# A recurrent block and a 32-expert layer on one core: first steps reordered, a fifth set of result buffers for expert 7, and both pairs of expert 0 added ahead of the last four scatters

## The reference

```
combined = xn @ W_in + b_in             # 256 embedding columns, 8 state columns
gate = sigmoid(combined @ W_g + b_g)
state[t] = gate[t] * state[t-1] + (1 - gate[t]) * state_in[t]
s = concat(embed, states) @ W_out + b_out

scores = softmax(xn @ wg.T)             # 32 experts in 8 groups; 4 groups kept, 4 experts chosen
w = chosen scores / their sum
y[token] += w * (silu(xe @ w1[e]) * (xe @ w3[e])) @ w2[e]    # at most 1280 rows an expert
z = (silu(xn @ sw1) * (xn @ sw3)) @ sw2                      # shared expert, all tokens
f = y + z
```

## Time and profile before

| quantity | value |
|---|---|
| median of 3 runs | 1074.14 us (1073.2 to 1076.17) |
| the profiled execution | 1077.56 us, its span 1075.8 us |
| instructions | 29677 |
| busy share: PE, PEld, DVE, ACT, POOL | 93%, 89%, 72%, 51%, 68% |
| mean granted clock of TensorE | 0.972 |

### The profile page before, as it was taken

One profiled execution on the slowest core, in us unless ns is written; L12 is line 12 of the kernel. 1 busy time (PEld: TensorE's weight loads), 2 busy tenths in 40 slices (PEclk: granted clock), 3 DMA queues, 4 the chain that ended last, 5 costly groups with the idle time before them and its releaser, 6 DMA issues.

```text
span 1075.8 us, 29677 instructions
## 1 busy us (share of the span) xinstructions
PE 1001.6 (93%) x8031; PEld 955.9 (89%) x8031; DVE 775.6 (72%) x2475; ACT 549.5 (51%) x1039; POOL 726.3 (68%) x572
## 2 busy tenths in 40 slices
PE   7879999998979997997999999999999999999965
PEld 6878898888879997997999999999999999999822
DVE  6778898887868874765677667767667777767674
ACT  4657786877654442443344344444444444444444
POOL 3066777777777776777888887666666666665440
PEclk8889999999999999999999999999999999999997
DMA  9933433443357878997899988988788988878879
GB/s 257 285 120 130 145 141 141 143 145 140 141 159 250 261 230 169 207 181 144 161 174 201 191 167 170 199 184 179 168 201 184 211 191 190 170 141 179 217 204 340
DMA packets 179346, 199.28 MB, mean 185 GB/s; under 512 B 20737, under 2 KB 171058, under 8 KB 179250
## 3 DMA queue, kind: packets, MB, share of 16 engines
q1 hardware_dynamic: 124992, 126.70, 39.6%
q0 software_dynamic: 53664, 71.50, 35.0%
q10 hardware_dynamic: 594, 0.01, 0.0%
HBM read 96.89 MB, written 104.90 MB: 188 GB/s over the span
## 4 chain that ended last, share of the span: by engine, by line
PE 55%; POOL 19%; issue 12%; DMA 6%; DVE 3%; ACT 2%; SPq 1%; POOLq 1%; DVEq 0%; ACTq 0%
POOL slot_rows L900 16%; PE h L1072 10%; PE h L1074 10%; PE h L1073 10%; PE yb L1090 5%; PE yb L1092 5%; PE yb L1091 5%; PE xt L1056 5%; POOL y_sum L883 4%; DMA y_sum<-y_more,y_idx 2%; DMA x_all<-slot_rows 1%; DMA y_sum<-x_all 1%; DMA y_sum<-yw,y_idx 1%; DVE s_all L2103 1%; DMA w_hl<-y_sum 1%
## 5 line engine op out<-in xcount | busy, mean ns | idle before, releaser
L1072 PE MATMUL h<-xh,w_hl 128*128 (+1 forms) x1392 | 410.4, 295 | 3.6 <-DVE xl L1698 2.0
L1074 PE MATMUL h<-xl,w_hl 128*128 (+1 forms) x1392 | 393.5, 283 | 0.0
L1073 PE MATMUL h<-xh,w_hl 128*128 (+1 forms) x1392 | 392.1, 282 | 0.0
L1422 ACT ACTIVATE acth<-act 128x512 fp32r<-128x512 f32 x174 | 109.9, 632 | 346.3 <-PE yb L1092 306.0
L1072 PEld LDWEIGHTS h<-xh,w_hl 128*128 128x128 f32 x1392 | 264.0, 190 | 5.5 <-issue 5.0
L1073 PEld LDWEIGHTS h<-xh,w_hl 128*128 128x128 f32 x1392 | 264.3, 190 | 0.0
L1074 PEld LDWEIGHTS h<-xl,w_hl 128*128 128x128 f32 x1392 | 263.5, 189 | 0.0
L1708 DVE TENSOR_TENSOR actl<-act,acth 128x512 fp32r<-128x512 f32 x174 | 120.6, 693 | 173.7 <-ACT acth L1422 173.2
L1090 PE MATMUL yb<-w_hl,acth 128*128 128x256 f32 x692 | 199.7, 289 | 8.6 <-DVE x_all L1977 6.3
L883 POOL DMA_INDIRECT y_sum<-x_all,y_idx x98 | 156.0, 1592 | 69.1 <-DVE x_all L1977 42.2
L1092 PE MATMUL yb<-w_hl,actl 128*128 128x256 f32 x692 | 197.5, 285 | 0.0
(11 more groups left out here) (253 smaller groups left out, 1606.0 us busy)
## 6 DMA issues: line engine op xcount, KB each, us to landing
rows<-slot_rows SPq DMA_DIRECT2D x122, 289.0 KB, 4.2
raw<-L_ffn_w SPq DMA_DIRECT2D x99, 256.0 KB
slot_rows<-rows SPq DMA_DIRECT2D x32, 289.0 KB
x_all<-L_attn_x SPq DMA_DIRECT2D x16, 512.0 KB, 9.3
x_all<-L_attn_x SPq DMA_DIRECT2D x32, 256.0 KB
out<-s_all SPq DMA_DIRECT2D x32, 256.0 KB, 3.7
y_sum<-yw SPq DMA_DIRECT2D x31, 256.0 KB
x_all<-slot_rows SPq DMA_DIRECT2D x20, 289.0 KB, 4.5
```

The source lines that it names most:

```text
L1072: mm(out, high, xh[:, k, cols], start=(k == 0), stop=False)
L1073: mm(out, low, xh[:, k, cols], start=False, stop=False)
L1074: ins = mm(out, high, xl[:, k, cols], start=False, stop=(k == KD - 1))
L1422: av(acth[:, :], act[:, :], ACT.Copy).then_inc(acth_ready, 2)
```

## The change

On SP, the stores of z of steps 0, 1 and 2 stand between the last six loads of x instead of behind them, and the stores of steps 28 and 29 stand behind the row loads of the first two early pairs. On DVE, the statistics of group 5 move from step 2 to step 1 (ahead of the recurrence), those of group 7 from behind the routing of step 3 to ahead of its recurrence, and the counts of step 29 from ahead of the recurrence to behind it. On PE, the product for these counts moves ahead of the gate products. On POOL, the adds of (0,0) and (0,1) stand ahead of the last four scatters.

A fifth set of result buffers, `SET_E`, lies in the first 2560 words of x and is used by expert 7 alone, without a wait. Expert 8 has set B, 9 C, 10 D, 11 A, and so on to expert 19; from 20 on A and B are used. The sections of experts 6 to 11 are straight code, 12 to 19 the loop. x is loaded again in another order: chunks 5 to 12, then 0 to 4 (from expert 14 on, with a wait for expert 9's first add), then the rest.

```diff
-SETS = 4
-CYCLE_END = 18
+SETS = 5
+CYCLE = 4
+CYCLE_START = 8
+CYCLE_END = 20
+KEPT_START = 14
...
-        y_flat += set_c + set_d + extra_y
+        y_flat += set_c + set_d + [x_words[:, n * 2 * D:(n + 1) * 2 * D] for n in range(SET)] + extra_y
-        SET_A, SET_B, SET_C, SET_D, EXTRA = (n * SET for n in range(SETS + 1))
+        SET_A, SET_B, SET_C, SET_D, SET_E, EXTRA = (n * SET for n in range(SETS + 1))
+        CYCLE_SETS = (SET_B, SET_C, SET_D, SET_A)
-            return (SET_A, SET_B, SET_C, SET_D)[(e - FIRST) % SETS] if e < CYCLE_END else (SET_B, SET_A)[e % 2]
+            if e < CYCLE_START:
+                return (SET_A, SET_E)[e - FIRST]
+            return CYCLE_SETS[(e - CYCLE_START) % CYCLE] if e < CYCLE_END else (SET_B, SET_A)[e % 2]
...
-            for g in range(10, GROUPS):
-                load_x(g)
 
             def store_z(q):
                 sp.wait_ge(z_ready, 2 * q + 2)
                 sp.dma_start(y_dram[bass.ds(q * PAIR, PAIR), :].rearrange("(t p) c -> p t c", p=P),
                              yw[:, :, :]).then_inc(z_stored, 16)
 
-            with sp.Fori(0, A_PAIRS - 2) as q:
+            for g in range(10, GROUPS):
+                if g % 2 == 0:
+                    store_z(g // 2 - 5)
+                load_x(g)
+            with sp.Fori(3, A_PAIRS - 4) as q:
                 store_z(q)
...
             sp.wait_ge(counts_ready, 1)
             for q in range(2):
                 load_early(q)
+                store_z(A_PAIRS - 4 + q)
...
-            with sp.Fori(FIRST, CYCLE_END) as e:
+            with sp.Fori(FIRST, KEPT_START) as e:
+                section(e)
+                load_x_again(e - FIRST + SET)
+            sp.wait_ge(first_added, first_adds(KEPT_START - SET))
+            with sp.Fori(KEPT_START, KEPT_START + SET) as e:
+                section(e)
+                load_x_again(e - KEPT_START)
+            with sp.Fori(KEPT_START + SET, KEPT_START + SET + 3) as e:
                 section(e)
                 load_x_again(e - FIRST)
-            sp.wait_ge(first_added, first_adds(CYCLE_END - 6))
-            with sp.Fori(CYCLE_END, CYCLE_END + 4) as e:
-                section(e)
-                load_x_again(e - FIRST)
...
                 slot = g % SLOTS
                 hold(dispatch_ready, GT * g + GT)
                 for t in range(GT):
+                    if g == GROUPS - 1 and t == GT - 1:
+                        pool.wait_ge(z_stored, 16 * (A_PAIRS - 1))
+                        pool.wait_ge(last_z_stored, 16)
+                        add_early(0)
+                        add_early(1)
                     for k in range(K):
                         pool.indirect_dma_start(
                             slot_table, bass.IndirectOffsetOnAxis(dest_idx[slot][:, t, k:k + 1], 0),
                             rows[slot][:, t, :], None, bounds_check=slot_bound, oob_is_err=False
                         ).then_inc(scattered[slot], 16)
-            pool.wait_ge(z_stored, 16 * (A_PAIRS - 1))
-            pool.wait_ge(last_z_stored, 16)
-            add_early(0)
-
...
-            add_early(1)
             pool.wait_ge(fifth_added, 32)
...
+                        pe.wait_ge(early_seen, GROUPS - 2)
+                        pe.wait_ge(pos_taken, GROUPS - 2)
+                        mm(cnt_early, ones[:, 0:1], seen_early[:, 1:GROUPS - 1, :].rearrange("p g e -> p (g e)"),
+                           start=True, stop=True).then_inc(cnt_ready, 1)
                     if has_next:
                         gate_inputs(p + 1)
                     else:
...
-                        pe.wait_ge(early_seen, GROUPS - 2)
-                        pe.wait_ge(pos_taken, GROUPS - 2)
-                        mm(cnt_early, ones[:, 0:1], seen_early[:, 1:GROUPS - 1, :].rearrange("p g e -> p (g e)"),
-                           start=True, stop=True).then_inc(cnt_ready, 1)
 
                 up(p, w_hl[1], region(i), meanwhile)
...
                     states_low(p + 1, 1 - i)
-                    if g == 0:
-                        statistics(4)
-                    if g == 1:
-                        statistics(5)
-                        statistics(6)
+                    if g in (0, 1):
...
                         norm_finish(norm_chunk(g + 2))
-                    if p == A_PAIRS - 3:
-                        count_early()
-                        mark_late()
                     if has_next:
+                        if g in (0, 1):
+                            statistics(5 + 2 * g)
                         if 2 <= g < 10:
                             statistics(g + 6)
                         if g in (5, 9):
                             variances(norm_chunk(g + 3))
                         recurrence(p + 1, 1 - i, g % BATCH_GROUPS == BATCH_GROUPS - 1)
+                    if p == A_PAIRS - 3:
+                        count_early()
+                        mark_late()
                     if has_next:
...
                         route_chosen(g)
                     if g == 1:
-                        statistics(7)
                         variances(norm_chunk(g + 3))
                     if p - 1 in FIRST_SPLITS:
                         n = FIRST_SPLITS.index(p - 1)
...
 
-                if e < FIRST + SETS:
+                if e == FIRST + 1:
+                    return None, 0
+                if e < CYCLE_START + CYCLE - 1:
                     of, j = EARLY_LIST[1 if e == FIRST else 2 + y_set(e) - SET_B + slot]
                     return ((first_added, first_adds(FIRST)) if of == FIRST - 1 else
                             (third_added[of % 2], third_adds(of)) if j == 2 else (apart_added[of], early_adds(of)))
                 if slot == 0:
-                    return first_added, first_adds(e - (3 if e == CYCLE_END else 5))
+                    return first_added, first_adds(e - (5 if e == CYCLE_START + CYCLE - 1 else 4 if e == CYCLE_END else 2))
                 return added[y_set(e) // SET][slot], slot_adds(slot, set_uses(e))
 
             def late_free(e):
...
                 pair(PAIRS, 1, (FIRST - 2, SET_A + PAIRS, fifth_added, 32), slot=PAIRS)
-            for e in range(FIRST, FIRST + SETS):
+            for e in range(FIRST, CYCLE_START + CYCLE):
```

More of the change, by code:

```diff
@@ L341, in build @@
         y_ready = sem("y_ready")
-        added = [[sem(f"added{n}_{slot}") for slot in range(PAIRS)] for n in range(SETS)]
+        added = [[None] + [sem(f"added{n}_{slot}") for slot in range(1, PAIRS)] for n in range(SETS)]
         first_added = sem("first_added")
@@ L442, in set_uses @@
         def set_uses(e):
-            return (e - FIRST) // SETS if e < CYCLE_END else (e - CYCLE_END) // 2 + (CYCLE_END - FIRST) // SETS
+            if e < CYCLE_START:
+                return 0
+            if e < CYCLE_END:
+                return (e - CYCLE_START) // CYCLE + (y_set(e) == SET_A)
+            return (e - CYCLE_END) // 2 + (CYCLE_END - CYCLE_START) // CYCLE + e % 2
         def first_adds(e):
@@ L977, in _ @@
                 pool.reg_mov(fifth_behind, 1)
-            for e in range(FIRST, FIRST + SETS):
+            for e in range(FIRST, CYCLE_START + CYCLE):
                 section(e, y_set(e), y_set(e - 1) if e > FIRST else None, set_uses(e - 1) + 1)
-            with pool.Fori(0, (CYCLE_END - FIRST) // SETS - 1) as i:
-                for n in range(SETS):
-                    section(i * SETS + FIRST + SETS + n, n * SET, (n - 1) % SETS * SET, i + 1 if n == 0 else i + 2)
+            with pool.Fori(0, (CYCLE_END - CYCLE_START) // CYCLE - 1) as i:
+                for n in range(CYCLE):
+                    section(i * CYCLE + CYCLE_START + CYCLE + n, CYCLE_SETS[n], CYCLE_SETS[n - 1], i + 2)
             for e in range(CYCLE_END, CYCLE_END + 2):
@@ L985, in _ @@
             with pool.Fori(0, (E - 2 - CYCLE_END - 2) // 2) as i:
-                section(i * 2 + CYCLE_END + 2, SET_B, SET_A, i + 4)
+                section(i * 2 + CYCLE_END + 2, SET_B, SET_A, i + 5)
                 section(i * 2 + CYCLE_END + 3, SET_A, SET_B, i + 5)
@@ L1914, in _ @@
                     states_low(p + 1, 1 - i)
-                    if g == 0:
-                        statistics(4)
-                    if g == 1:
-                        statistics(5)
-                        statistics(6)
+                    if g in (0, 1):
+                        statistics(4 + 2 * g)
                     if p == A_PAIRS - 2:
@@ L2028, in body @@
                     if slot == PAIRS:
-                        if isinstance(e, int) and e < FIRST + SETS:
+                        if isinstance(e, int) and e < CYCLE_START + CYCLE - 1 and e != FIRST + 1:
                             ve.wait_ge(*waits(slot))
@@ L2062, in _ @@
                 pair(PAIRS, 1, (FIRST - 2, SET_A + PAIRS, fifth_added, 32), slot=PAIRS)
-            for e in range(FIRST, FIRST + SETS):
+            for e in range(FIRST, CYCLE_START + CYCLE):
```

(12 more changed lines are left out.)

13 lines of the change are left out of this document (6 added, 7 removed).

## The result

The changed kernel took 1062.97 us (median of 4 runs, 1059.69 to 1066.98) beside 1074.41 us before; the ratio is 0.9902, with a 95% interval of 0.9876 to 0.9929. That is 10.5 us less (0.0098 of 1074.41), where 7.3 us were forecast. The intervals overlap, so the gain lies between about 7 and 11 us; the lower of these is the forecast. The profiled execution took 1065.27 us, its span is 1063.5 us, 12.3 us shorter than that of before.

A forecast was written before the change was run, and what follows sets the result against it. Outside its holes PE is full; POOL's queue place sets the holes near 403.5 and 503.5 us. Gain -8.1 at 503.5, +0.8 at 403.5: 7.3 us, from 1074.14 to 1066.8 us, range 1063.2 to 1071.8.

The forecast's parts named there:

- Step 1's delay: DVE's step 1 gets a 1.74 us statistics block where it idles 1.15 us: group 0's indices come 0.6 us later.
- S: Time by which POOL's scatter chain starts earlier: taken as 6.0 us, between -0.6 and 8.2.
- the rival in which no gap is left: PE keeps its clock in step 4, POOL alone limits: S = 8.2, gain 9.5, 1064.6 us; chance 0.20.
- The z store: Step 2: ScalarE's 3.78 us wait for the first z store goes, but PE's last product limits the gain to 0.8 us.
- The statistics: Steps 2 and 3: statistics blocks moved off the path give 1.9 us each, plus about 0.9 through PE's clock.
- L: Landing time of the last scatter behind the four adds: between 0 and 4.3 us, taken as 3.0.
- x: How much earlier PE gets the rows of (5,3): S - L - 3.8 = -0.8 us, slightly later.
- What the adds give back: POOL's third pair of adds starts at 404.9 to 406.4, the adds running 8.9 to 10.4 us earlier from there.
- The hole at 503.5: PE's loss at expert 8's fifth pair, a wait on a count of adds, goes whatever S is: 8.1 us.
- The wait for (5,3): PE's wait for expert 5's fourth pair grows from 5.2 to about 16 us, as PE comes some 10 us earlier.
- The loop's jump: DVE's jump back comes after expert 15 instead of 13, at the same price, 3.6 us of PE.
- The rival in which the ask for (5,3) runs away: SP's ask waits behind adds and a stretched landing: x = -12.3 against 8.1, 1078.3 us; chance 0.06.

The follow-up runs named there:

- e5: Kernel before, with the fifth pairs of experts 7 to 9 waiting for their own buffer's early pair instead of the count: 1066.97 us, 0.9956.
- e2: Kernel before, with the first-step edits and the adds ahead of the last four scatters, still four result sets: 1064.52 us, 0.9911.
- e3: Changed kernel with the four adds of expert 0 put back behind the last scatter: 1069.76 us, 0.9954.
- e1: Kernel before, with only the first-step edits on SP, DVE and PE, nothing on POOL: 1071.14 us, 0.9966.
- e6: Changed kernel with expert 0's adds behind the last scatter and fifth pairs of experts 7 to 10 waiting for their own buffer alone: 1058.22 us, 0.9875.
- e7: Changed kernel with expert 0's adds behind the last scatter and POOL's flag load ahead of its wait for those adds: 1064.16 us, 0.9921.
- e9: Changed kernel, adds left in place, with fifth pairs of experts 7 to 10 waiting for their own buffer alone: 1063.48 us, 0.9931.
- e11: e6 with DVE's sections of experts 12 to 19 written out instead of looped: 1051.05 us, 0.9831 to the kernel before.
- e4: Changed kernel with the first steps as before (z stores, statistics, counts): 1075.12 us, 1.0013.
- e10: Changed kernel with all z stores behind all x loads as before, stores of steps 28 and 29 also put back: 1067.66 us, 0.9962.
- e8: Changed kernel with the statistics of groups 4 to 7 in their earlier places: 1068.88 us, 0.9975.

## Why the prediction was right, and where its steps were off

The direction, the places and the order of size were right, and the range, laid on the measured ratio (0.9902 x 1074.14 = 1063.6 us), held the time, near its lower end. That the number came so near is in part luck: over the runs the hole was worth 4.7 us and not 8.1 (e5), and (5,3) came 3.84 us earlier in the profile and not 0.8 later, and the two errors work against each other. Step by step:

- **Step 1's delay**: 0.6 us forecast, and group 0's scatters began at 51.24 for 50.64. The match is luck, as this start moves by more between executions with the same first steps: 49.55 in e2 and 54.36 in e3, and 48.95 in e5 with those of before.
- **S, the earlier scatters**: right for group 1 (72.1 forecast, 72.40 measured) and near for group 2 (93 to 96; 94.22, so S is 7.1 and not 6.0). Other executions with the new first steps (e1, e2, e3, e6, e7, e9, e11) have group 2 at 91.94 to 97.78, e4 and e5 with the old ones at 102.99 and 99.96, so the sign is firm and the size loose. With one gap of 0.79 us left, this is nearly the rival in which no gap is left; in e6, e7 and e9 none is, and there PE had, as that rival asks, its full clock in step 4 (1.00 from 70 to 80 us, for 0.83 in the changed kernel and 0.71 before).
- **The z store, 0.8 us**: mis-sized. e10 gives 3.3 to 6.4 us for it, with the stores of steps 28 and 29. The copy itself went as the step said: in e9 PE's last product ends its wait, and it starts at 51.95 where the step had 52.0 (e10: 53.48). In the changed kernel, whose PE had run at full clock from 30 to 50 us, it starts at 50.57. What the step left out came behind the copy: in e10 PE's clock from 70 to 80 us is 0.67, and the gap before group 2 is 3.34 us as in the earlier trace rows, where e9 has 1.00 and no gap. That the late copy brings this spell on was not tried by itself. Nor was what decides the clock from 30 to 50 us: it was 1.00 in e5, with the old first steps, too.
- **The statistics, 4.7 us with PE's clock, less 0.6**: the mechanism was right, the size in the profile too (e8 has 4.6 us of gaps for 0.8), and the runs give 4.7 to 7.8. In e8's execution group 0 happened to begin 2.1 us earlier than in the changed kernel's, so that group 2 was only 1.7 us later.
- **L, the landing behind the adds, 3.0 us**: mis-sized, and it set the sign of x. From the last scatter's end to the ask it took 1.77 us, so L is 0.9 with the 0.9 that SP was given. Four adds in front don't stretch it: with them in front it was 1.77 to 3.21 us (the changed kernel, e2, e4, e8 to e10), without them 2.11 to 3.24 us (e1, e3, e6, e7, e11; in e3 and e6 SP's zero stores ended 1.2 us behind the last scatter and may have held the ask, the other three have 2.31 to 3.24). The bound taken from the earlier trace rows was that of adds, which the scatters don't share. So (5,3) came 3.84 us earlier where 0.8 us later was forecast: 2.1 us of this are L and 1.1 us S, the transfer itself was 0.6 us shorter (3.79 for 4.43), and the last scatter ended 0.8 us earlier than S and the 7.4 us of the adds make it.
- **What the adds give back**: the two terms were read well, their place was wrong. In the kernel before the fourth add landed after 5.9 us and 3.5 us followed, one of the two ends that the step gave; e3 and e7 have 6.4 and 6.3 us of landing, 2.4 us of load and 1.0 us behind both. But the step let the flags begin at the last scatter's end. In the changed kernel they passed beside the last two scatters, so the third pair stood 0.58 us behind the last scatter, at 400.12 and not at 404.9 to 406.4. This made no difference to the sum, as the hole goes with either.
- **The hole at 503.5, 8.1 us**: gone as forecast, and none follows at expert 9. That it is a count was right (e5). Its price over the runs is 4.7 us (3.3 to 6.2); the profiled execution showed more.
- **The wait for (5,3) grows to about 16 us**: it grew to 13.23 us, as the rows came earlier than forecast (PE came 11.9 us earlier, where some 10 were forecast).
- **The fifth result set and the unrolled sections count for nothing**: right (e2).
- **The loop's jump at the same price**: nearly. It moved to expert 15's end; PE did 176 instructions in 635 to 660 where a full stretch has 215, 39 x 0.117 = 4.6 us for 3.6 before.

The rival in which the ask for (5,3) runs away had its place right, and e4 is that case: without the first steps (5,3) moves back by 6.5 us, and all that the hole gave is lost. Its price of 12.3 us was too high, as L in e4 is 3.21 - 0.9 = 2.3 and not 5.9. What the sum did not say is that the parts need each other: it adds S whether or not the adds move, and e1 shows S worth only 3.6 us while the hole is there, since POOL stands at other waits on its way to it. e4's first gap of 9.55 us, 3.4 us more than in the earlier trace rows for the same code there, goes with ACT's wait for the first z store, which was 3.78 us in the earlier trace rows (e5, with the same first steps, has a wait of 5.04 us and a gap of 7.63):

```profile
54.67 0.60 ACT L1444 ACTIVATE yw<-yb 128x512 f32<-128x512 f32 x1 [6.86 <-DMA y_sum<-yw]
```

Why that wait differs from execution to execution stays open.

## What to carry to other kernels

When two waits hang on one queue, an edit that shortens what comes before one of them may only lengthen the other; time the parts alone and together. Before work is moved ahead of a critical transfer to clear a later wait, ask whether the later wait needs what it waits for: here a wait on a count, for a buffer that was long free, could simply be narrowed, and that gave 4.7 us alone and 13 us with the first steps, against 6.0 us paid for the move. Let an engine's wait, and the register load behind it, pass beside work that the engine has already been given: here POOL's load of the flags cost 0.3 us at most beside two scatters, and 2.4 us where POOL had nothing else under way.

## What was not expected of the hardware

- The jump back of DVE's loop over four sections idled DVE for 2.71 us before and 3.69 us after (2.62 to 4.59 in all runs that have it), and cost PE 3.6 to 5.0 us with its lower clock (before, after and e6); the same sections in straight code cost nothing that shows (e11). DVE's later loop, over two sections, jumps back without such an idle: behind 700 us DVE has no idle over 0.5 us that the profile puts down to issue, before or after. What makes the difference was not tried.
- The same add by index, the second of pair (0,1), landed 4.0 us after its start in the changed kernel, 5.9 us before and 6.4 us in e3. POOL, waiting for it, took 1.0 us more to start the next (e7).
- The first 100 us differ from run to run by the granted clock: the same edits gave 1.00 in the changed kernel and 0.84 in e1 and e9 from 30 to 50 us, and 1.00 and 0.83 (e1) from 50 to 60 us. The changed kernel's runs spread over 7 us (1059.69 to 1066.98).
